# Splitting the projected keys of a two-layer perceiver into bf16 parts: subtractions on TensorE in PSUM instead of on VectorE and GpSimd

## The reference, cut to what matters

```
x = x + xattn0(LN(x), ctx)    # per query and head: keep 32 of 6272 scores, softmax, context -> FiLM scale/shift,
                              # S4D (through an FFT), norms, one MLP, final norm
x = x + gla(LN(x))            # gated linear attention with a cumulative sum, 3-tap convolution
x = x + moe0(LN(x))           # sigmoid router, 2 of 8 experts, plus a shared expert
x = x + xattn1(LN(x), ctx)    # 16 heads of 8 over all 6272 context rows:
                              #   kh = ctx @ Wk + bk;  vh = ctx @ Wv + bv;  softmax(qh kh^T * scale) vh;  @ Wo + bo
x = x + attn1(LN(x))          # causal self-attention over the 64 tokens
x = x + moe1(LN(x))           # softmax router, 2 of 8 experts
```

## Time and profile before

| | us |
|---|---|
| median of 3 runs | 322.18 (321.97 to 328.8) |
| the profiled execution's own time | 320.57 |
| its span, first to last instruction | 318.8 |
| PE busy | 244.7 (77%) |
| DVE busy | 195.1 (61%) |
| ACT busy | 146.7 (46%) |
| POOL busy | 66.1 (21%) |
| mean granted TensorE clock | 0.855 of full speed |

### The profile page before, as it was taken

The page is one execution under the profiler, slowest core; times in us unless marked ns, Lnnn a source line. Parts: engine busy times, 40 slices in busy tenths (PEclk is TensorE's granted clock), DMA queues, the critical chain, the costliest instruction groups (busy, mean ns, idle before and its releaser), DMA issues.

```text
span 318.8 us, 5155 instructions
## 1 busy us (share of the span) xinstructions
PE 244.7 (77%) x2021; PEld 149.7 (47%) x2042; DVE 195.1 (61%) x482; ACT 146.7 (46%) x234; POOL 66.1 (21%) x97
## 2 busy tenths in 40 slices
PE   1995852596998658959777988998998888784884
PEld 1342312485873323424554855665665556431422
DVE  3299997898925464435236567776776770224464
ACT  1788930883623425235236575465565556301030
POOL 4895897002000442430013000000000000000000
PEclk9999595776999575558999999999999999757599
DMA  7992001000077000000089999999999509000000
GB/s 203 281 384 93 1 0 31 38 2 0 2 296 296 0 0 0 0 3 0 2 105 124 101 131 122 107 122 123 105 109 120 59 19 373 9 0 0 0 2 4
DMA packets 3807, 26.84 MB, mean 84 GB/s; under 512 B 1212, under 2 KB 1405, under 8 KB 2184
## 3 DMA queue, kind: packets, MB, share of 16 engines
q1 hardware_dynamic: 3784, 26.52, 42.1%
HBM read 16.85 MB, written 0.03 MB: 53 GB/s over the span
## 4 chain that ended last, share of the span: by engine, by line
PE 31%; DVE 9%; issue 5%; ACT 4%; POOL 1%; DVEq 0%; POOLq 0%; ACTq 0%
PE B L1039 17%; PE A L1039 12%; DVE mx L930 3%; ACT probs L606 1%; PE B L1337 1%; ACT mid L597 1%; DVE moe_w L927 1%; ACT moe_w L588 0%; ACT L606 0%; DVE m L969 0%; DVE probs L970 0%; DVE s L973 0%; POOL ctxn L434 0%; POOL ctxn L436 0%; DVE probs L962 0%
## 5 line engine op out<-in xcount | busy, mean ns | idle before, releaser
L930 DVE TENSOR_REDUCE mx<-B 128x1 f32<-128x512 f32 (+1 forms) x104 | 65.1, 656 | 26.2 <-PE B L1039 22.1
L606 ACT ACTIVATE probs<-A 128x896 f32<-128x896 f32 x56 | 51.3, 918 | 37.1 <-PE A L1039 36.8
L343 POOL TENSOR_TENSOR rstd<-ve,mhalf 64x1 f32<-64x1 f32 x10 | 5.5, 546 | 206.0 <-DVE ve L639 204.6
L1039 PE MATMUL B<-probs,scores 128*32 128x128 f32 x736 | 34.0, 280 | 4.9 <-ACT mid L597 3.5
L1039 PE MATMUL A<-ctxT,qq 98*128 98x512 f32 (+1 forms) x52 | 27.4, 690 | 5.4 <-ACT scores L464 4.9
L1039 PE MATMUL B<-scores,moe_w 128*128 128x512 bf16 (+2 forms) x118 | 29.2, 344 | 2.7 <-DVE mx L930 1.0
L1039 PEld LDWEIGHTS B<-probs,scores 128*32 128x32 f32 x736 | 19.2, 109 | 11.4 <-ACT probs L606 6.7
L673 DVE MAX8 mid<-scores 128x8 f32<-128x128 f32 x98 | 19.4, 279 | 4.5 <-ACT scores L464 4.5
L1039 PE MATMUL A<-ctxT,blob_l 98*128 98x512 f32 (+1 forms) x26 | 19.4, 879 | 3.4 <-DVE probs L779 3.4
L1039 PEld LDWEIGHTS A<-ctxT,qq 98*128 98x128 f32 x52 | 11.5, 232 | 21.8 <-issue 11.4
L1039 PE MATMUL A<-moe_w 112*128 112x128 bf16 (+2 forms) x146 | 19.8, 281 | 0.8 <-DVE moe_w L927 0.7
(11 more groups left out here) (347 smaller groups left out, 395.0 us busy)
## 6 DMA issues: line engine op xcount, KB each, us to landing
ctxT<-scores SPq DMA_DIRECT2D x20, 196.0 KB, 7.3
ctxn<-in_ctxn SPq DMA_DIRECT2D x1, 2352.0 KB, 8.2
moe_w<-in_moe_w SPq DMA_DIRECT2D x1, 2304.0 KB, 8.2
ctxn<-in_moe_w SPq DMA_DIRECT2D x1, 2304.0 KB, 9.0
scores<-in_e_gu SPq DMA_DIRECT2D x1, 2048.0 KB, 8.5
ctxn<-scores SPq DMA_DIRECT2D x10, 196.0 KB, 7.3
moe_w<-scores SPq DMA_DIRECT2D x10, 196.0 KB, 6.9
ctxT<-in_ctxT SPq DMA_DIRECT2D x3, 588.0 KB
```

Source lines behind the costliest of these rows:

```text
L343: nc.gpsimd.tensor_tensor(rstd[:, :], ve[:, :], mhalf[0:T, :], ALU.pow).then_inc(S["rstd_ready"], 1)
L606: A_(probs[:, (n % RING) * 1024:(n % RING) * 1024 + w], A[:, 2 * (n % 2):2 * (n % 2) + 2, :].rearrange("p a b -> p (a b)")[:, 0:w], ACT.Ex ...
L930: V.tensor_reduce(mx[:, m, t:t + 1], bank[:, 0:SB0[t][1]], AX_X, ALU.max).then_inc(S["max_used"], 1)
L1039: return mm(out_, lhsT, rhs, start=start, stop=stop)
```

## The change: what it does

- The residual stays in PSUM. After `key_hi` PE adds minus the identity (bf16, `neg_id`) times the hi part to the same PSUM bank, ACT evacuates the bank as mid, PE subtracts that in the same way, ACT evacuates it as low. DVE's `key_rest` and POOL's `key_low` are gone; a tile is now 3 TensorE operations and 3 ScalarE evacuations, in a software pipeline over tiles.
- Tiles 0 to 3 are made between the last score tile and the flag matmul of `top32`, in banks B2, B3, A3, B0, and are kept in a new buffer `k_early`. Tiles 4 to 12 stay in the middle stage, over the four banks of `A`. ACT holds the early tiles ahead of `ztop`.
- Before the first `moe_up` PE now waits for the last low part.
- Each of the six stack copies is two DMAs: columns of `k_early` and the rest.
- `ctxT`, `wk1` and `wv1` are padded with zeros from 98 to 128 rows; the pad of `ctxT` is one more DMA behind `blob_l`, ahead of `ctxn`.
- `scaled_norm` replaces `layernorm` plus two or three operations in two places; one new POOL operation computes x + b_out ahead (`x0b`).
- The copy `kf` goes from DVE to ACT, behind the last attention evacuation. The one-row matmul of `film_b` (512 columns) goes from behind `values` to behind the transposes of group 11.

```diff
+K_EARLY = 4
-K_AT = {"film": (0, 1), "xf": (1, 2), "y": (2, 4), "up": (4, 5), "mlp": (5, 8), "gla": (8, 11), "moe": (11, 13)}
-K_LOW = [(3, 0), (4, 4), (5, 4), (6, 9), (None, 13)]
+K_AT = {"early": (0, 6), "film": (4, 5), "xf": (5, 6), "y": (6, 8), "up": (8, 9), "mlp": (9, 11), "gla": (11, 12), "moe": (12, 14),
+        "route": (14, 15)}
...
                 for row, kp in STACK:
-                    sp.dma_start(slot[row:row + PAIR, :], kpart[kp][PAIR * m:PAIR * (m + 1), :]).then_inc(stack_ld[m % 4], 16)
+                    e = K_EARLY * BANK
+                    sp.dma_start(slot[row:row + PAIR, 0:e], early_part[kp][PAIR * m:PAIR * (m + 1), :]).then_inc(stack_ld[m % 4], 16)
+                    sp.dma_start(slot[row:row + PAIR, e:G], kpart[kp][PAIR * m:PAIR * (m + 1), e:G]).then_inc(stack_ld[m % 4], 16)
...
+            tt(x0b[:, :], W["x"], W["b_out"], ALU.add).then_inc(S["pool_const"], 1)
...
-                tt(kpart[2][:, s:s + w], krest[:, n % 2, 0:w], kpart[1][:, s:s + w], ALU.subtract).then_inc(S["k_low"], 1)
...
+            def key_hi(n):
+                act.wait_ge(S["k_ps"], n + 1)
+                A_(key_tile(0, n), key_bank(n), ACT.Copy).then_inc(S["k_hi"], 1)
+            def key_mid(n):
+                act.wait_ge(S["k_rest"], n + 1)
+                A_(key_tile(1, n), key_bank(n), ACT.Copy).then_inc(S["k_mid"], 1)
+            def key_low(n):
+                act.wait_ge(S["k_left"], n + 1)
+                A_(key_tile(2, n), key_bank(n), ACT.Copy).then_inc(S["k_low"], 1)
+            def keys_at(place):
+                lo, hi = (0, K_EARLY) if place == "early" else (K_EARLY, len(SB0))
+                for i in range(*K_AT[place]):
+                    if i < hi:
+                        key_hi(i)
+                    if i - 2 >= lo:
+                        key_low(i - 2)
+                    if lo <= i - 1 < hi:
+                        key_mid(i - 1)
+            keys_at("early")
...
+            def scaled_norm(dst, part, src, g, b):
+                link(V.bn_stats(st[:, :], src))
+                link(V.bn_aggr(mv[:, :], st[:, :]))
+                V.tensor_scalar_add(ve[:, :], mv[:, 1:2], EPS_LN).then_inc(S["var_ready"], 1)
+                norm[0] += 1
+                link(V.scalar_tensor_tensor(part, src, mv[:, 0:1], g, ALU.subtract, ALU.mult))
+                dve.wait_ge(S["rstd_ready"], norm[0])
+                link(V.scalar_tensor_tensor(dst, part, rstd[:, :], b, ALU.mult, ALU.add))
...
-                    V.tensor_tensor(krest[:, n % 2, 0:w], A[:, n % 2, 0:w], kpart[0][:, s:s + w], ALU.subtract)\
-                        .then_inc(S["k_rest"], 1)
...
+            def key_raw(n):
+                if n >= K_EARLY + 4:
+                    pe.wait_ge(S["k_low"], n - 3)
+                if n == K_EARLY + 3:
+                    pe.wait_ge(S["kf_sb"], 1)
+                s, w = SB0[n]
+                one(key_bank(n), W["wk1"], ctxT[:, s:s + w]).then_inc(S["k_ps"], 1)
+            def key_minus(n, i, done, left):
+                pe.wait_ge(S[done], n + 1)
+                mm(key_bank(n), neg_id[:, :], key_tile(i, n), start=False, stop=True, skip_group_check=True).then_inc(S[left], 1)
+            def project_keys(place):
+                lo, hi = (0, K_EARLY) if place == "early" else (K_EARLY, len(SB0))
+                for i in range(*K_AT[place]):
+                    if i < hi:
+                        key_raw(i)
+                    if i - 2 >= lo:
+                        key_minus(i - 2, 1, "k_mid", "k_left")
+                    if lo <= i - 1 < hi:
+                        key_minus(i - 1, 0, "k_hi", "k_rest")
+            pe.wait_ge(S["ld_l"], 32)
+            pe.wait_ge(S["const_ready"], 2)
+            project_keys("early")
...
-            keep_clock_up("route")
-            pe.wait_ge(S["k_rest"], len(SB0))
+            project_keys("route")
+            pe.wait_ge(S["k_low"], len(SB0))
             moe_up(0)
```

More of the change, by code:

```diff
@@ L280, in chunk_cols, with key_tile, key_bank @@
             return t[:, c * P:(c + 1) * P]
+        early_part = [k_early[:, i * K_EARLY * BANK // 2:(i + 1) * K_EARLY * BANK // 2].bitcast(BF16) for i in range(3)]
+        def key_tile(i, n):
+            s, w = SB0[n]
+            return (early_part[i] if n < K_EARLY else kpart[i])[:, s:s + w]
+        def key_bank(n):
+            bank = [B[2], B[3], A[:, 3, :], B[0]][n] if n < K_EARLY else A[:, n % 4, :]
+            return bank[:, 0:SB0[n][1]]
         ctx_cuts = [0, 3 * BANK, 6 * BANK, 9 * BANK, G]
@@ L766, in _ @@
                                            ALU.mult, ALU.add).then_inc(S["film_row"], 1)
[L768 to L778, removed]
-                    V.tensor_tensor(krest[:, n % 2, 0:w], A[:, n % 2, 0:w], kpart[0][:, s:s + w], ALU.subtract)\
-                        .then_inc(S["k_rest"], 1)
+                    scaled_norm(xin[:, :], nt[:, :], x0[:, :], W["g_in"], W["b_in"])
             dve.wait_ge(S["c2T_ps"], 1)
@@ L840, in _ @@
             V.tensor_tensor(glob[:, :], us[:, :], ge4[:, :], ALU.mult).then_inc(S["glob_ready"], 1)
-            key_rest("gla")
             dve.wait_ge(S["blk1_ps"], 1)
@@ L892, in add_pair @@
                 return acc[:, p % 2, :]
-            key_rest("moe")
-            dve.wait_ge(S["ld_l"], 16)
+            dve.wait_ge(S["ld_l"], 32)
             V.tensor_scalar(hm[:, :], W["mask_h1"], W["scale1"], None, ALU.mult)
@@ L1115, in _ @@
                     values(b - 2)
+                if b == len(GROUPS) - 2:
+                    pe.wait_ge(S["film_row"], 1)
+                    one(B[3][0:T, :], one_at["film_b"][:, 0:T], W["film_1"], stop=False)
                 if b in SPECTRUM_AT:
@@ L1134, in project_values @@
                 for i, c in enumerate(V_BANKS[b]):
-                    last = one(v_bank(b)[:, i * V_ROW:(i + 1) * V_ROW], chunk_cols(ctxT[0:KA, :], c), W["wv1"])
+                    last = one(v_bank(b)[:, i * V_ROW:(i + 1) * V_ROW], chunk_cols(ctxT, c), W["wv1"])
                 last.then_inc(S["v1_ps"], 1)
-            def project_keys(place):
-                for n in range(*K_AT[place]):
-                    s, w = SB0[n]
-                    if n >= 2:
-                        pe.wait_ge(S["k_rest"], n - 1)
-                    one(A[:, n % 2, 0:w], W["wk1"], ctxT[0:KA, s:s + w]).then_inc(S["k_ps"], 1)
             pe.wait_ge(S["cT_sb"], 1)
@@ L1515, in lay_out @@
     w["wr"], w["norm_wT"] = m1["Wr"], m1["norm_w"].T
+    for n in ("wk1", "wv1"):
+        w[n] = np.concatenate([w[n], np.zeros((P - KA, w[n].shape[1]), np.float32)], 0)
     out = {}
@@ L1528, in lay_out @@
     out["dft_k"] = w["dft_k"]
+    out["pad"] = np.zeros((P - KA, G), np.float32)
     out["fill"] = np.concatenate([np.full((1, G // 2), 0x3F803F80, np.uint32), np.zeros((15, G // 2), np.uint32)], 0).view(np.float32)
```

83 lines of the change are left out of this document (29 added, 54 removed).

## The result

The changed kernel takes 305.88 us (median of 4 runs, 304.64 to 307.01) against 322.25 us for the kernel before beside it: ratio 0.949 [0.945, 0.954], 16.4 us less. Forecast were 310 and a range of 301 to 317. The profiled execution took 307.01 us, span 305.1, 13.6 less than the 320.57 of before; it is the longest of the four, so I compare stages inside the two profiles and times by the medians. Some executions of one and the same kernel come out over 1.5% longer than its shortest, at a lower granted clock; the ratios leave them out, the medians and ranges do not.

What follows compares the result with a forecast made beforehand. Head-pair loop near full; target was the serial middle, 93 to 141 us, its 64-token chain delayed by key-split work. -0.35 - 10.55 - 1.4 = -12.3 gives 308.3 profiled, 310 median; main case 306 to 314, overall 301 to 317.

Steps and rivals of the forecast that it cites:

- A: Main case: middle stage stays at half clock after the change, granted clock near 0.5 from about 105 to 135; chance 0.50.
- Early tiles: Four key tiles in the idle stretch 44.6 to 54.1 us: cost 0, bounds 0 and +1.5 us.
- First attention: Attention up to FiLM: folded norm -0.7, `film_b` matmul moved in +0.9, c2T transpose freed -0.55; sum -0.35 us.
- FiLM to inverse transform: Middle stage: `key_rest` 0 and `kf` leave VectorE's list, -1.0 us.
- Norm to `w1`: Middle stage: norm falls from 1.27 to 0.34 us and `hT` stops waiting; `w1` starts at 104.0, not 106.84: -2.8.
- `up` to the MLP's end: Middle stage: one tile as before plus two bf16 passes, +0.9, leaving -2.0 us at the MLP's end.
- `ut`: After the final norm, TensorE with two tiles in front reaches it at 116.35, not 121.47 us: -5.1.
- `moe_up`: End of the router: TensorE's 3.22 us wait for `key_rest` 12 becomes 0.8 us for low 12: -10.55.
- Behind it: Expert stage, value projection and loop shift unchanged; padding, pad load, `x0b` and the doubled stack DMAs cost 0.
- D: Rival: split stack copies arrive late in the head-pair loop; at 0.6 us per added DMA, +21 us, 331; chance 0.08.
- C: Rival: ScalarE's chained evacuations bind the middle stage, 5.1 us lost, 316 with early tiles' +1.5; chance 0.16.
- B: Rival: clock stays high, middle stage runs at 2.4 GHz, 9.1 us more gained, time 301; chance 0.22.

Runs made afterwards that it cites:

- the run of the small edits: Kernel before with only gain and bias folded into two norms, the `kf` copy on ScalarE and `film_b`'s matmul inside the attention: 322.86 us, ratio 1.001.
- the moved norm: Changed kernel with the negated identity on ScalarE, plus the norm of xin moved behind VectorE's last attention group: 298.79 us, ratio 0.929; repeated, 295.77 us, 0.914.
- its own neighbour: Changed kernel with the negated identity made by ScalarE instead of VectorE, norm of xin not moved: 303.64 us, ratio 0.929.

## Why the forecast was right, and where it was not

The direction and the size were right: 12.3 us less were forecast, the two profiles differ by 13.56. That the sum is so near is in part luck, because three errors nearly cancel: the start of the stage came 1.1 us later than forecast, the stage gained 4.7 us more, and 2.3 us were lost behind it. The main case (A, the stage at half clock from 105 to 135) is not what happened. By item:

- **Early tiles, 0: right.** Twelve evacuations lie between 46.4 and 54.1 us, TensorE's last subtraction starts at 53.1. The flag matmul slipped to 55.13, under the bound of 55.5, behind VectorE and not behind the keys; why POOL's chain ended later stayed open. It stands outside of the sum.
- **First attention, -0.35:** the FiLM matmul came 0.76 us later, not 0.35 earlier; the attention's own part was met. VectorE began group 0 at 59.18 us, not 57.98, and 0.4 of these 1.2 us came back up to the FiLM matmul. The late head was not foreseen.
- **FiLM to inverse transform, -1.0:** the inverse transform starts 3.91 us behind the FiLM matmul, 4.72 before: -0.8.
- **Norm to `w1`, -2.8:** 8.97 us for 11.54, -2.6; norm at 0.34 us, TensorE's wait for a mid evacuation 0.38 where I took 0.45.
- **`up` to the MLP's end, -2.0:** `w2` starts at 11.71 us, not 15.87: -4.2; VectorE takes its result at 12.84, not 17.87: -5.0. Here the failed step begins.
- **`ut`, -5.1:** 16.78 for 26.17: -9.4. I had TensorE take two tiles in front at 5.4 us; it took 3.4 at full clock (108.79 to 112.2, with a wait of 0.38) and then waited 0.65 for VectorE.
- **`vT`, -8.1:** -14.1. **`moe_up`, -10.55 and -1.4 of clock:** -16.65. From `ut` to `moe_up` the gain is 7.3 us, 5.45 forecast with another 1.4 for the clock: nearly met.
- **Behind it, 0:** +2.3, of which 1.8 is the value projection (5.01 us for 3.22), where the clock fell at 142.9.
- **D** fell by two runs (the loop's 92 us in the changed kernel, and the split copies alone), though the 8 us that its sum takes off 48 p stood there without a row. **C** fell by TensorE's 1.5 us of waits for mid parts, under my bound of 3; without the early tiles it is 3.1. **A and B** each describe half of the stage: full clock to 115.6, half from there to `moe_up`.

The step that failed is the one of the stage's clock: "I keep the rest at half clock, because in 124.4 to 128.0 TensorE was busy 3.60 of 3.60 us and the clock still stayed at 0.50". The row showed that a clock that has fallen does not come back at once under dense work. It did not show that the clock would fall in the new order. In the kernel before it fell at 104.8, at the end of this wait of TensorE for `hn` (its trace, in time), and in the run of the split copies, which has the same order, at 105.4 behind the same 1.74 us:

```profile
104.76 0.29 PE L1167 MATMUL B<-blob_a,hn 64*128 64x64 f32 x1 [1.74 <-DVE hn L644]
```

The change fills this wait and takes the 1.78 us for `hT` behind it down to 0.44; the clock stayed full, and the sum was short by 4.3 us up to `ut`. The run that fills only the waits of the old kernel agrees from the other side: with 0.23 us of wait there, the fall came only at 114.8, in a wait of 4.42 us. That is the support for the wait as the cause, and it is not the whole of it: in the run of the small edits the clock fell at 96.3, and in two profiles of one program it fell at 112.6 or not at all, each time behind short waits that other runs passed at full clock. Which wait lets the clock fall is not settled. The Trainium skill (TensorE: Matmul & The Clock Gate, Part 1) says that sustained activity releases the throttle; for the fall in the wait for `hn` these runs agree, for the way back the half-clock stretch of that run, 17.22 of 17.80 us busy at 0.50, does not.

What made the stage 16.65 us shorter: ten more us of full clock alone brought 2.0 in the old order, and the small edits alone nothing (47.26 us, at 0.55). The new subtraction alone brought 12.9 (with the clock at 1.00, not 0.64), the early tiles alone 8.9 (at 0.61, in the run of 317.0 us). That points to work taken out of the lists of VectorE, POOL and ScalarE for most of it, and to the clock for the rest. The two were not measured apart, since each change of order moved the clock too.

## What to carry to other kernels

A serial stage with work of other streams in its lists is priced by its lists, but its clock must be forecast for the new order: ask which wait of TensorE stood ahead of the fall and whether the change removes it, and give both clocks a chance, because the same program showed both. A row at half clock prices the stay at half, not the fall. Judge a further edit against the version that has everything but that edit: the moved norm looked like 4 to 7 us against the changed kernel, and its ratio beside its own neighbour was the same, 0.929.

## What the runs showed of the hardware

- Two DMAs of 64 and 132 KB from 16 partitions cost no more than one of 196 KB (ratio 0.997 [0.991, 1.003] with 48 more of them), and landed in 4.3 and 4.5 us, not 7.3 (medians, changed kernel).
- A bf16 subtraction through the identity, 128x512, took 0.38 us alone at full clock and 0.63 at half; an eviction of 128x512 to bf16 0.60 us.
- The same program's granted clock differs between executions: `moe_up` came 28.90 and 27.84 us into the stage in two profiles of the changed kernel, 25.92 and 27.53 in two of the version with the late norm, and four runs of the one with the negated identity on ScalarE took 297.9 to 308.1 us. The part behind the loop took 46.2 us at clock 0.74 and 42.3 at 0.83.
- The `hn` norm operation took 1.27 us beside POOL's subtractions, three times in the kernel before, and 0.34 without them, three times in the changed kernel.
